# GpSimd computes the inverse square roots of the second attention's two norms, and the first guess takes one operation in place of two

## What is computed

```python
def _layernorm(x, axis=-1, eps=1e-05):
    m = jnp.mean(x, axis=axis, keepdims=True)
    v = jnp.var(x, axis=axis, keepdims=True)
    return (x - m) / jnp.sqrt(v + eps)

h = _L0_tok_ref(x, L0_tok_weight)
h = h + _L0_attn_ref(_layernorm(h, axis=-1), ...)
h = h + _L0_ffn_ref(_layernorm(h, axis=-1), ...)
h = h + _L1_attn_ref(_layernorm(h, axis=-1), ...)
h = h + _L1_ffn_ref(_layernorm(h, axis=-1), ...)
```

## Time and profile before

| what | value |
|---|---|
| median of 3 runs | 2872.7 us (2871.28 to 2873.52) |
| the profiled execution's own time | 2848.83 us |
| its span in the trace | 2847.1 us |
| TensorE busy | 2329.4 us, 82% |
| VectorE busy | 1953.5 us, 69% |
| ScalarE busy | 1717.9 us, 60% |
| GpSimd busy | 1180.3 us, 41% |

### The profile page before, as it was taken

One profiled execution on the slowest core, in us unless ns is written; L12 is line 12 of the kernel. 1 busy time (PEld: TensorE's weight loads), 2 busy tenths in 40 slices (PEclk: granted clock), 3 DMA queues, 4 the chain that ended last, 5 costly groups with the idle time before them and its releaser, 6 DMA issues.

```text
span 2847.1 us, 56530 instructions
## 1 busy us (share of the span) xinstructions
PE 2329.4 (82%) x15787; PEld 2060.0 (72%) x15787; DVE 1953.5 (69%) x8789; ACT 1717.9 (60%) x5240; POOL 1180.3 (41%) x1217
## 2 busy tenths in 40 slices
PE   4888863367676599999999899999989999998584
PEld 4777753255555388888888798999978898987463
DVE  3666767754444288989889877777778877878111
ACT  4666655321221277777777778887867787776242
POOL 6444500178888502222222234444446543644332
PEclk9888975587777799999999999999999999999555
DMA  2222310044444520000000155555447754752565
GB/s 74 73 73 73 90 53 0 10 76 70 77 76 71 108 51 26 29 24 25 26 29 24 37 145 143 152 144 141 120 143 205 200 146 127 211 159 79 139 192 167
DMA packets 282600, 271.20 MB, mean 95 GB/s; under 512 B 32796, under 2 KB 232058, under 8 KB 282289
## 3 DMA queue, kind: packets, MB, share of 16 engines
q1 hardware_dynamic: 236208, 206.42, 26.6%
q0 software_dynamic: 46080, 61.16, 9.4%
HBM read 182.69 MB, written 86.84 MB: 95 GB/s over the span
## 4 chain that ended last, share of the span: by engine, by line
PE 48%; DVE 24%; POOL 11%; issue 8%; ACT 3%; DMA 3%; another core or an unknown queue 2%; SPq 2%; DVEq 0%; POOLq 0%
POOL hbuf L779 7%; PE bank L2014 5%; PE bank L1977 5%; PE bank L2061 5%; PE bank L2022 4%; PE bank L2047 4%; PE bank L1985 4%; POOL xe L771 3%; PE bank L1976 3%; DVE junk L1284 3%; PE bank L1997 3%; PE bank L1999 2%; PE bank L1998 2%; DVE pr_place L1480 2%
## 5 line engine op out<-in xcount | busy, mean ns | idle before, releaser
L819 POOL DMA_INDIRECT spread_rows<-kb,pos x256 | 249.1, 973 | 523.0 <-ACT pr_place L1032 338.8
L833 POOL DMA_INDIRECT zbuf<-pc,kb x288 | 288.9, 1003 | 377.7 <-DVE pc L1642 317.4
L1977 PE MATMUL bank<-xT,gT 128*128 128x256 f32 x1024 | 308.2, 383 | 0.0
L1030 ACT ACTIVATE pr_place<-bank,nmax 128x128 f32<-128x128 f32 x512 | 188.4, 368 | 185.1 <-DVE nmax L1462 171.1
L1985 PE MATMUL bank<-ident,pr_place 128*128 128x128 f32 x1536 | 256.9, 277 | 43.4 <-DVE pr_place L1480 42.2
L1461 DVE TENSOR_REDUCE nmax<-bank 128x1 f32<-128x128 f32 x512 | 142.9, 279 | 216.3 <-PE bank L1977 123.6
L1985 PEld LDWEIGHTS bank<-ident,pr_place 128*128 128x128 f32 x1536 | 189.8, 141 | 137.7 <-DVE pr_place L1473 67.2
L1480 DVE COPY pr_place<-bank 128x384 f32<-128x384 f32 x512 | 280.3, 547 | 6.1 <-PE bank L1985 3.2
L2061 PE MATMUL bank<-wvo_part,x_part 128*128 128x512 f32 x768 | 270.6, 461 | 0.0
L1040 ACT ACTIVATE bank<-causal 128x384 f32<-128x384 f32 x512 | 253.4, 495 | 19.8 <-PE bank L2099 3.7
L2047 PE MATMUL bank<-x_part,wqk_part 128*128 128x256 f32 x1536 | 246.9, 297 | 1.7 <-DVE x_part L1587 1.2
(11 more groups left out here) (301 smaller groups left out, 6454.3 us busy)
## 6 DMA issues: line engine op xcount, KB each, us to landing
pa<-bundle SPq DMA_DIRECT2D x288, 321.0 KB
kb<-spread_rows SPq DMA_DIRECT2D x288, 65.0 KB
junk<-zbuf SPq DMA_DIRECT2D x32, 512.0 KB
xrow<-xr SPq DMA_DIRECT2D x32, 320.0 KB
hbuf<-h SPq DMA_DIRECT2D x32, 256.0 KB
hx<-hbuf SPq DMA_DIRECT2D x64, 128.0 KB
h3buf<-h SPq DMA_DIRECT2D x64, 128.0 KB
pc<-h3buf SPq DMA_DIRECT2D x32, 256.0 KB
```

The source lines that it names most:

```text
L819: pool.indirect_dma_start(out=spread_rows, out_offset=bass.IndirectOffsetOnAxis(ap=pos[:, k, j:j + 1], axis=0), in_=xr4s[g % 2][:, k, j], ...
L833: pool.indirect_dma_start(out=zbuf, out_offset=bass.IndirectOffsetOnAxis(ap=xu[:, t % XR, C + 1:XW].bitcast(U32), axis=0), in_=yu[:, t % Y ...
L1977: pe.matmul(s2[:, P:3 * P], g[:, P:2 * P], xT3[:, p], start=False, stop=True, skip_group_check=True)\
```

## The change

GpSimd gets an `inv_sqrt` of its own, of 15 operations, since the last operation of a Newton step is made as two (an addition and a product). `prep_root` and `gate_root` now stand in GpSimd's list: `prep_root(0)` ahead of the slots, `prep_root(n + 1)` at h = 1 behind `residual` and ahead of the scatter, and `gate_root` at (0, 5). VectorE signals with `var3_ready` and `var4_ready` that the variances are there, and waits on `root3_step` in `prep_norm` (slot 3) and on `root4_step` in `gate_norm` (slot (0, 7)). The last gate's root, in the tail, stays on VectorE. VectorE's own `inv_sqrt`, used in layer 0 and by the last gate, makes the first guess with one integer operation (times -0.5, plus the constant) in place of a shift and a subtraction, so it has 12 operations.

```diff
+            ROOT = 15
+
+            def inv_sqrt(sem_done, base, v, y, t, h):
+                for k in range(ROOT):
+                    if k not in (0, 2):
+                        pool.wait_ge(sem_done, base + k)
+                    if k == 0:
+                        ins = pool.tensor_scalar(h, v, EPS, None, ALU.add)
+                    elif k == 1:
+                        ins = pool.tensor_scalar(y.bitcast(I32), h.bitcast(I32), -0.5, float(0x5F3759DF), ALU.mult, ALU.add)
+                    elif k == 2:
+                        ins = pool.tensor_scalar(h, h, -0.5, None, ALU.mult)
+                    elif k % 4 == 3:
+                        ins = pool.tensor_tensor(t, y, y, ALU.mult)
+                    elif k % 4 == 0:
+                        ins = pool.tensor_tensor(t, t, h, ALU.mult)
+                    elif k % 4 == 1:
+                        ins = pool.tensor_scalar(t, t, 1.5, None, ALU.add)
+                    else:
+                        ins = pool.tensor_tensor(y, t, y, ALU.mult)
+                    ins.then_inc(sem_done, 1)
+
+            def prep_root(n):
+                pool.wait_ge(var3_ready, n + 1)
+                if n >= 1:
+                    pool.wait_ge(xn3_ready, n)
+                inv_sqrt(root3_step, ROOT * n, mv3[:, :, 1], r3[:, 0], r3[:, 1], r3[:, 2])
+
+            def gate_root(g):
+                pool.wait_ge(var4_ready, g + 1)
+                if g >= 1:
+                    pool.wait_ge(xn4_ready, g)
+                inv_sqrt(root4_step, ROOT * g, mv4[:, :, 1], r4[:, 0], r4[:, 1], r4[:, 2])
+
+            prep_root(0)
             for u in range(NB * H1):
                 n, h = u // H1, u % H1
                 i, p = n // 2, n % 2
                 if h == 0:
                     residual(n)
+                if h == 1 and n + 1 < NB:
+                    prep_root(n + 1)
                 if i >= 2 and 1 <= h <= TG:
                     pool.wait_ge(exp_ready, u - 1)
                     scatter(i - 2, p, h - 1)
+                if (p, h) == (0, 5) and i >= 1:
+                    gate_root(i - 1)
...
-            ROOT = 13
+            ROOT = 12
...
-                    ins = dve.tensor_scalar(t.bitcast(U32), h.bitcast(U32), 1, None, ALU.logical_shift_right)
+                    ins = dve.tensor_scalar(y.bitcast(I32), h.bitcast(I32), -0.5, float(0x5F3759DF), ALU.mult, ALU.add)
...
             def prep_norm(n, p):
-                prep_now["steps"].wait()
+                dve.wait_ge(var3_ready, n + 1)
+                dve.wait_ge(root3_step, 15 * (n + 1))
...
             def gate_norm(g):
                 gate_steps["now"].wait()
+                dve.wait_ge(var4_ready, g + 1)
+                if g < NG - 1:
+                    dve.wait_ge(root4_step, 15 * (g + 1))
...
-                        root_step()
                         if there(u - N_LAG):
                             inverses(u - N_LAG, (h - N_LAG) % H1)
```

More of the change, by code:

```diff
@@ L372, in lm_tower @@
         w_c = sem("w_c")
+        var3_ready = sem("var3_ready")
+        var4_ready = sem("var4_ready")
+        root3_step = sem("root3_step")
+        root4_step = sem("root4_step")
         masked = sem("masked")
@@ L1124, in stats @@
                 steps.done(ins)
-            ROOT = 13
+            ROOT = 12
             def inv_sqrt(k, steps, v, y, t, h):
-                if k != 3:
+                if k != 2:
                     steps.wait()
@@ L1134, in inv_sqrt @@
                 elif k == 1:
-                    ins = dve.tensor_scalar(t.bitcast(U32), h.bitcast(U32), 1, None, ALU.logical_shift_right)
+                    ins = dve.tensor_scalar(y.bitcast(I32), h.bitcast(I32), -0.5, float(0x5F3759DF), ALU.mult, ALU.add)
                 elif k == 2:
-                    ins = dve.tensor_scalar(y.bitcast(I32), t.bitcast(I32), -1.0, float(0x5F3759DF), ALU.mult, ALU.add)
-                elif k == 3:
                     ins = dve.tensor_scalar(h, h, -0.5, None, ALU.mult)
+                elif k % 3 == 0:
+                    ins = dve.tensor_tensor(t, y, y, ALU.mult)
                 elif k % 3 == 1:
-                    ins = dve.tensor_tensor(t, y, y, ALU.mult)
-                elif k % 3 == 2:
                     ins = dve.tensor_tensor(t, t, h, ALU.mult)
@@ L1426, in _ @@
             serve(NU - 1, True)
-            PREP = 2 + 1 + 13
+            PREP = 2
             prep_now = {}
@@ L1442, in prep_stats @@
                     ins = dve.bn_aggr(mv3[:, j], st3[:, j])
[L1443 to L1448, removed]
+                ins.then_inc(var3_ready, 1)
             def prep_norm(n, p):
-                prep_now["steps"].wait()
+                dve.wait_ge(var3_ready, n + 1)
+                dve.wait_ge(root3_step, 15 * (n + 1))
                 if not first(n):
@@ L1496, in gate_stats, with last_root @@
                     ins = dve.bn_aggr(mv4[:, j], st4[:, j])
[L1497 to L1502, removed]
+                ins.then_inc(var4_ready, 1)
+            def last_root():
+                n_ = gate_steps["now"]
+                dve.wait_ge(var4_ready, NG)
+                for k in range(ROOT):
+                    inv_sqrt(k, n_, mv4[:, :, 1], r4[:, 0], r4[:, 1], r4[:, 2])
             def gate_norm(g):
                 gate_steps["now"].wait()
+                dve.wait_ge(var4_ready, g + 1)
+                if g < NG - 1:
+                    dve.wait_ge(root4_step, 15 * (g + 1))
                 hh = h3[:].rearrange("p q j c -> p (q j) c")
@@ L1589, in _ @@
             prep_stats(0, 0, 0)
-            for k in range(ROOT):
-                prep_root(k)
             prep_norm(0, 0)
@@ L1650, in slots @@
                         u = H1 * n + h
[L1652 to L1662, removed]
                         if (p, h) == (1, 7) and there(i - 1):
@@ L1717, in _ @@
             gate_stats(NG - 1)
-            for k in range(ROOT):
-                gate_root(k)
+            last_root()
             gate_norm(NG - 1)
```

## The result

| | median us | runs |
|---|---|---|
| before | 2872.48 | 4 (2871.28 to 2873.52) |
| changed | 2952.03 | 4 (2943.39 to 2955.11) |

The ratio is 1.0269, 95% interval [1.0248, 1.0291]: slower by 79.6 us, where 12.6 us faster was forecast. The same two kernels run in another session gave 0.9934 [0.9909, 0.9958], faster by 21 us (e5). The loss came back in a third session (e9); the gain was measured in one. Most of what follows is about that difference.

The account below looks back on a forecast made before the run. TensorE and VectorE were taken as nearly even in rounds 1 to 14, TensorE as binding later; -3.0 + 2.0 - 12.6 - 2.5 + 3.5 = -12.6 us gave 2860 us, range 2848 to 2867.

Parts of the forecast that it names:

- Rounds 15 to 31, "+3.5 (0 to +25)" for GpSimd's own load: Unit rounds: GpSimd 72% loaded, roots queued behind transfers late for VectorE; +3.5 us, range 0 to +25.
- Rounds 1 to 14, "-12.6": Rounds without expert units: lighter VectorE frees TensorE's waits, 0.9 us a round; -12.6 us, ends -5.6 and -18.8.
- the cap of 1.34: Slots (0, 4) to (0, 6): three TensorE waits for VectorE's copy, at most 1.34 us a round to gain.
- The parts that I named (1.09 us): Per round, rounds 1 to 14: nine gate operations off VectorE's path 0.63 us, shorter L1473 as `hb` moves 0.46 us.
- the 0.2 taken off for meetings on the port: Rounds 1 to 14: GpSimd's small products meet VectorE's scalings, costing 0.2 us a round, range 0 to 0.7.
- A root of 4.7 us on GpSimd: Each root moved to GpSimd takes 4.7 us, between 3.0 and 9.5, extrapolated from larger operations.
- rival 1: Gate's norm: GpSimd's root too slow, VectorE and those behind wait; about +30 us (2903), chance 0.12.
- `hb` moves away from L1473: Slot (0, 4): sum queued behind the gate's root, so L1473 gets 0.46 us shorter, 0.81 to 0.35.
- rival 3: Scalings under a gate's root: shared port holds them up 1.4 us; -1 to +5 us overall (2875), chance 0.12.
- Layer 0 and the first norm, -3.0 and +2.0: Layer 0: one operation less per root, -3.0 us; first norm of the slots: slower exposed GpSimd root, +2.0 us.
- Rounds 15 to 31, -2.5: Unit rounds: TensorE's wait for VectorE's copy shrinks, -2.5 us of at most -6.4.
- the second, "GpSimd falls behind in the unit rounds": Unit rounds: transfers ahead of `add_rows` and GpSimd's load make roots late; about +8 us (2881), chance 0.10.

Follow-up runs that it names:

- e5: The changed kernel, unaltered, against the kernel before, in a session without waits of unknown signal: ratio 0.9934 [0.9909, 0.9958].
- e9: The changed kernel, unaltered, against the kernel before (2875.28 us), in a session with waits of unknown signal: ratio 1.0269 [1.0244, 1.0293].
- prompt session: Kind of session in which no trace has a wait of unknown signal; the kernel before has a median of 2780 to 2781 us.
- late session: Kind of session in which every trace has waits of unknown signal; the kernel before has a median of 2845 to 2875 us.
- e8: The kernel before, unaltered, run for its trace in a session without waits of unknown signal: 2782.99 us.
- e1: The kernel before with only the one-operation first guess, all roots left on VectorE: ratio 0.9984 [0.9974, 0.9994].
- e3: The kernel before with the one-operation guess and only the gate's root on GpSimd: ratio 0.9915 [0.9898, 0.9931].
- e4: The kernel before with the one-operation guess and only attention's root on GpSimd, ahead of the scatters: ratio 0.9973 [0.9962, 0.9984].
- e12: The kernel before with each sequence's four scatters back to back, in a session with waits of unknown signal: ratio 1.0560 [1.0532, 1.0588].
- e2: The kernel before with each sequence's four scatters back to back, in a session without waits of unknown signal: ratio 1.0049 [1.0032, 1.0065].

## Why the prediction was wrong

**What failed** is the sum's last pair of terms and one condition of the third.

- *Rounds 15 to 31, "+3.5 (0 to +25)" for GpSimd's own load.* In the first pair these rounds cost 80.2 us more (1061.9 - 981.7). This is the mis-sized term. I read the load as lateness of the roots, and named as its mark a wait of L1510 or L1455 for GpSimd. In the changed kernel's trace there is no such wait (the lines are L1551 and L1492 there) from 1100 to 1534 and from 1650 to 2700 us. What came late was results of other engines, while GpSimd issued its queued DMAs without a break, and with the waits came the lower clock. The step that failed is "roots queued behind one are late for VectorE": I asked what is queued ahead of a root, not what is queued behind it. The order of before and after showed `prep_root` ahead of the scatter of h = 1; with 4.4 us in front, the scatters of the next slots are all due when it ends.
- *Rounds 1 to 14, "-12.6".* In the prompt session 43.78 - 42.38 = 1.40 us a round, 19.6 us, a little above the cap of 1.34. The parts that I named (1.09 us) fall short of it even without the 0.2 taken off for meetings on the port, so some of this gain isn't accounted for. Attention's root, which I put at 0, gains 0.61 us a round alone (43.78 - 43.17) and nothing on top of the gate's (42.34). In the late session 0.06 us a round: the same gain, and 1.35 us lost again, in slots (0, 3) and (1, 3), where the scatters now bunch.

The warning stood in the trace of before. It has waits put down to "remote" too, nearly all in the units' rounds, and I read past them, as they named no engine of the change. VectorE and GpSimd there:

```profile
1669.58 0.17 DVE L1466 RECIPROCAL rinv<-rsum 128x2 f32<-128x2 f32 x1
1673.46 0.29 DVE L1461 TENSOR_REDUCE nmax<-bank 128x1 f32<-128x128 f32 x1 [3.71 <-remote]
...
1669.17 0.97 POOL L819 DMA_INDIRECT spread_rows<-kb,pos  x1 [2.84 <-issue]
1670.45 0.98 POOL L833 DMA_INDIRECT zbuf<-pc,kb  x1 [0.30 <-issue]
1671.74 0.97 POOL L819 DMA_INDIRECT spread_rows<-kb,pos  x1 [0.30 <-issue]
1673.01 0.98 POOL L833 DMA_INDIRECT zbuf<-pc,kb  x1 [0.30 <-issue]
```

Four DMAs in a row and a wait of 3.71 us. The units' rounds of before have 16 waits of the maxima that end at the fourth of such a run, 3.2 us in the mean, and 54 beside a single one or the first of a run, 1.2 us. In e8, the same kernel in a prompt session, two end at the fourth, 1.0 us. A change that queues scatters behind something else makes more of the first kind.

**What held.**

- *A root of 4.7 us on GpSimd.* Operations of one root of attention's norm, the first to the last, and then the sum `hb` and the gate's norm behind the gate's root that follows, in the changed kernel's rounds 1 to 14:

```profile
1303.51 0.22 POOL L848 TENSOR_SCALAR r<-mv 128x2 f32<-128x2 f32 x1 [12.18 <-DVE mv L1483]
...
1305.31 0.19 POOL L860 TENSOR_TENSOR r<-r 128x2 f32<-128x2 f32 x1
1305.58 0.19 POOL L854 TENSOR_TENSOR r<-r 128x2 f32<-128x2 f32 x1
...
1307.69 0.19 POOL L860 TENSOR_TENSOR r<-r 128x2 f32<-128x2 f32 x1
...
1320.24 0.73 POOL L831 TENSOR_TENSOR hb<-hx,bo 128x256 f32<-128x256 f32 x1
...
1320.57 1.25 DVE L1551 TENSOR_SCALAR kb<-h,mv,r 128x128 f32<-128x128 f32 x4
```

  The root takes 4.37 us. One small product is 0.19 to 0.20 us and starts 0.27 before the next, where I had 0.24 and 0.34. The gate's norm starts without a wait, so rival 1 fell.
- *`hb` moves away from L1473.* That of p = 1 now runs at the gate's norm, as forecast, and the longest scaling of 256 columns in ten rounds is 0.492 us where it was 0.816. In the prompt session (e5) only this one has moved: in rounds 1 to 14 13 of 224 scalings still take 0.8 us, where before (e8) 26 do.
- *The port (rival 3).* The scaling's median is 0.347 us against 0.346, with three GpSimd roots a round beside it, and the 58 of 160 scalings that overlap one of its two-input operations take 0.350 at most. The Trainium skill says in "Advanced Engine Details and Errata", section "VectorE Performance Modes", that GpSimd instructions and two-port VectorE instructions block each other. With operations of 2 or 4 columns that cost VectorE nothing measurable here. What delay there is falls on GpSimd: of its 40 small operations that took 0.29 us or more in these ten rounds, 30 overlap a scaling, of the other 408 it is 129.
- *Layer 0 and the first norm, -3.0 and +2.0.* e1, which has the shorter guess and nothing else, is 4.4 us faster (0.9984), in line with -3.0, though its slots have shorter roots too. e5 begins its slots 0.3 us earlier than e8, e3 and e4 1.8 and 3.5 us later, e1 6.6 us earlier. Starts scatter by as much as the terms, so neither is told apart by them, and the +2.0 stays untested.
- *Rounds 15 to 31, -2.5.* In the prompt session -3.1 (949.8 - 952.9), one execution each, and this holds the +3.5 as well, of which nothing shows there.

Of the rivals the second, "GpSimd falls behind in the unit rounds", named the place, at a third of the price and by another mechanism; its chance of 0.10 was for something else.

**What stays open.** Why sessions differ, and by what path a row of indirect DMAs holds back other engines' signals. The runs show when and how much, not what is shared. The packets of SyncE's queue took the share 24.6% of the span of e12 and 26.9% of e2's, which is 746 and 752 us, and GpSimd's issue of a scatter takes 970 and 972 ns: neither the transfers nor the issue got slower. A late session costs the kernel before more ahead of the slots, where the edit does next to nothing, than in the units' rounds: its first slot begins at 987.0 us against 949.6 in e8, 37.5 us, and 28.8 us are added in the units' rounds; the tail is the same (226.7 and 227.0). Also open is why in rounds 1 to 14 a burst without a root adds nothing.

## What to carry to other kernels

When work is put on an engine that also issues DMAs, list what is queued behind it and when each of those was due: if several are due when it ends, they leave as one burst. Put such work where one transfer at most waits for it, or cut it so that a piece stands between transfers (no version here that cut attention's root gained, but the loss of 3.0% fell to 0.7%), and read waits without a known releaser in the trace before as a warning of what a burst costs. Of the versions that were run in both kinds of session the gate's root alone on GpSimd is the one faster than the kernel before in both (0.9946 and 0.9915); and a change of this sort should be timed in more than one session, since this one has opposite signs in two.

## What the runs showed of the hardware

- The same program took 2780 us in some sessions and 2845 to 2875 in others, with spreads of 0.1 to 1.0% inside each, on one core and with nothing altered.
- In the longer ones four or more indirect DMAs issued by GpSimd 0.30 us apart go with waits of VectorE and ScalarE of up to 8.4 us, most of them for results of TensorE. The kernel with 29 runs of six or more takes 175 us more in the units' rounds there than elsewhere; elsewhere these runs cost 2 us (955.0 against 952.9).
- Such waits go with a lower granted clock of TensorE: in the units' rounds it was at its lower level for 24 us in the kernel before, 75 in the changed one and 142 in the burst (late sessions; 20 for the burst in a prompt one).
- A GpSimd operation on 2 or 4 columns takes 0.19 to 0.28 us in nine cases of ten, the longest 0.54, and two inputs are no dearer than one (medians 0.19 to 0.20 against 0.19 to 0.29).
